# Rewriting the first attention of a two-layer network in fp32: narrow products, another split of the work over the engines

## What is computed

```python
xn = layernorm(x, axis=-1)                    # over the 512 columns
q  = xn.reshape(B, 8, 32, 512);  k = v = ctx.reshape(B, 8, 32, 512)
qk = einsum('bhdq,bhdl->bhql', q, k) / sqrt(32)
sm = softmax(qk, axis=-1)                     # over the 512 keys
x  = x + gamma * einsum('bhql,bhdl->bhdq', sm, v).reshape(B, 256, 512)
```

## Time and profile before

| | us |
|---|---|
| median of 3 runs | 2164.12 (2162.57 to 2165.21) |
| profiled execution | 2165.63 |
| its span | 2163.8 |
| first transposed score of tile 0, of tile 15 | 45.38, 489.10 |
| first product of the next stage | 527.39 |

### The profile page before, as it was taken

The page is one execution under the profiler, slowest core; times in us unless marked ns, Lnnn a source line. Parts: engine busy times, 40 slices in busy tenths (PEclk is TensorE's granted clock), DMA queues, the critical chain, the costliest instruction groups (busy, mean ns, idle before and its releaser), DMA issues. The chain is left out here.

```text
span 2163.8 us, 33174 instructions
## 1 busy us (share of the span) xinstructions
PE 1887.0 (87%) x10911; PEld 876.8 (41%) x11054; DVE 1692.2 (78%) x3042; ACT 1262.2 (58%) x2016; POOL 794.7 (37%) x681
## 2 busy tenths in 40 slices
PE   3998888896699999799398999999999997869998
PEld 0433333332244443354253444444444443324444
DVE  6799999998826637388688999999999994684443
ACT  2666666654534625144146999999999994521211
POOL 3112222212514515000202888888888883000000
PEclk9999999998899999899698999999999998889999
DMA  6754334402000000110001555555555656000000
GB/s 136 231 115 87 72 67 84 84 9 81 0 0 1 0 0 1 65 33 29 25 0 40 108 108 104 108 108 108 108 105 109 108 106 219 5 1 20 20 20 20
DMA packets 343369, 143.06 MB, mean 66 GB/s; under 512 B 307408, under 2 KB 315600, under 8 KB 342096
## 3 DMA queue, kind: packets, MB, share of 16 engines
q1 hardware_dynamic: 343248, 141.51, 29.5%
HBM read 70.15 MB, written 4.19 MB: 34 GB/s over the span
## 5 line engine op out<-in xcount | busy, mean ns | idle before, releaser
L1385 ACT ACTIVATE a_prob<-a_psS,a_bias,q_scale 128x1024 uint8<-128x1024 f32 x512 | 610.6, 1209 | 26.6 <-PE a_psS L1278 25.6
L1314 DVE TENSOR_REDUCE a_tops<-a_psM 128x1 f32<-128x512 f32 x1024 | 622.7, 681 | 2.0 <-PE a_psM L1268 0.4
L1364 POOL CAST a_wide<-a_pairs 128x2048 int16<-128x2048 uint8 x256 | 481.0, 1894 | 97.3 <-DMA a_pairs<-a_prob 84.8
L1268 PE MATMUL a_psM<-KT,QO 128*128 128x512 bf16 x968 | 353.5, 387 | 16.0 <-DVE a_tops L1314 10.3
L1278 PE MATMUL a_psS<-KT,QO 128*128 128x512 bf16 x967 | 292.9, 380 | 6.6 <-ACT a_prob L1385 3.6
L561 PE MATMUL psO<-prob,vs 128*128 128x512 f32 x512 | 267.2, 604 | 25.3 <-ACT prob L361 20.6
L1290 PEld LDWEIGHTS a_psO<-V,a_wide 128*128 128x128 f16 x4096 | 175.3, 96 | 144.3 <-DVE QO L1327 23.0
L361 ACT ACTIVATE prob<-psT 128x512 f32<-128x512 f32 x256 | 150.7, 595 | 127.1 <-PE psT L549 113.4
L675 POOL TENSOR_TENSOR g_sum<-g_sum 128x512 f32<-128x512 f32 x88 | 126.9, 1442 | 196.9 <-DVE g_sum L740 196.9
L1290 PE MATMUL a_psO<-V,a_wide 128*128 128x32 bf16 x4096 | 181.3, 177 | 20.3 <-DVE QO L1327 15.6
L849 PE MATMUL g_psY<-raw_dn,g_hT 128*128 128x512 f32 x352 | 162.2, 622 | 26.2 <-DVE raw_dn L700 15.8
(11 more groups left out here) (194 smaller groups left out, 2892.4 us busy)
## 6 DMA issues: line engine op xcount, KB each, us to landing
xs<-in_x SPq DMA_DIRECT2D x64, 256.0 KB, 4.7
cs<-in_ctx SPq DMA_DIRECT2D x64, 256.0 KB, 7.7
KT<-in_w SPq DMA_DIRECT2D x2, 4096.0 KB, 21.0
raw_gu<-in_gu SPq DMA_DIRECT2D x4, 1408.0 KB, 17.4
vs<-in_ctxT SPq DMA_DIRECT2D x64, 64.0 KB, 2.2
k_cT<-in_ctxT SPq DMA_DIRECT2D x16, 256.0 KB, 2.7
a_pairs<-a_prob SPq DMA_TRANSPOSE x256, 2.7
out<-x_sb SPq DMA_DIRECT2D x16, 256.0 KB, 2.0
```

Of the source, the lines that this page charges most:

```text
L1268: pe.matmul(psM[n % NM][:, :], QOf[:, i * P:(i + 1) * P], KTf[:, keys:keys + 512], start=True, stop=True).then_inc(shown, 1)
L1314: v.reduce_max(tops[i // JOIN % NB][:, i % JOIN, c:c + 1], psM[n % NM][:, :], AX.X).then_inc(topped, 1)
L1364: pool.tensor_copy(wide[i % NV][:, :, :, :].rearrange("p k c q -> p k (c q)"), both).then_inc(widened, 1)
L1385: act.activation(prob[i % NP][:, k * HK:(k + 1) * HK], psS[g % NS][:, :], ACT.Exp, scale=q_scale[:, i:i + 1], bias=bias[i // JOIN % NB][:, ...
```

## The change

The interface stays. In `mix_rows`:

- weigh now issues, for each quarter c of the keys, four fp32 products with a 32-column stationary operand (the head's values) into the four 32-partition pieces of one `psO`, and four with 32 columns of ones into `psE`: eight products per quarter, 32 a tile, where there were 16 with 128 columns. The pieces are ordered by quarter and then by head, and `prob` has eight slots.
- normalising moves to ACT (`Identity` with scale and bias, L441). ACT masks keys and queries directly (L434, L450), with no separate high copy; the subtraction for `ks` and `qs` is on POOL, head by head (L363, L372). The Newton step goes to POOL (L346 to L355).
- the maxima are split by one cast on DVE and three steps on POOL. One transpose turns all 48 columns; `less` (51 by 128 for each piece, with minus ones) picks and subtracts them in four 128-column products (L621) in place of one with 512 columns. `psS` has three buffers.
- collect runs once a tile, on 128 partitions, inside the following tile. Queries and keys are prepared two tiles ahead (three buffers), statistics three ahead. Unpacking is spread over the last two tiles. The loop is written out, and `vs` is loaded by one DMA a tile.

```diff
-    FIRST = 6
+    RING = 2 * HT
+    FIRST, LEAD = 3, 3
@@ gpsimd
+            def queries(j):
+                if j >= 3:
+                    pool.wait_ge(tscored, NU * (j - 2))
+                for h in range(HT):
+                    pool.wait_ge(q_cut, 2 * j + h // 2 + 1)
+                    pool.tensor_tensor(qs[j % 3][:, h, :], xs[j % 3][:, h, :], q_sub[:, h, :],
+                                       ALU.subtract).then_inc(q_ready, 1)
...
+            def steps(j):
+                if has(j - 2):
+                    finish(j - 2)
+                if has(j + 2):
+                    keys(j + 2)
+                if has(j + 3):
+                    roots(j + 3)
+                if has(j + 1):
+                    split(j + 1)
+                if has(j + 2):
+                    queries(j + 2)
@@ scalar
+            def steps(j):
+                for n in range(NU):
+                    if has(j):
+                        exp(j, n)
+                    if n in (0, 1) and has(j + 2):
+                        cut_keys(j + 2, n)
+                    if n == HT - 1 and has(j - 1):
+                        collect(j - 1)
+                    if n == 5 and has(j + 3):
+                        roots(j + 3)
+                    if 6 <= n < 6 + HT and has(j + 2):
+                        normalise(j + 2, n - 6)
+                    if n in (10, 11) and has(j + 2):
+                        cut_queries(j + 2, n - 10)
@@ vector
+            def steps(j):
+                if has(j + 3):
+                    statistics(j + 3)
+                if has(j + 1):
+                    maxima(j + 1)
+                if has(j - 1):
+                    invert(j - 1)
+                if has(j + 1):
+                    maxima_rows(j + 1)
+                if has(j - 2):
+                    after(j - 2)
+                if j == NT - 2:
+                    move(0)
+                    move(1)
+                    mask(0)
+                    mask(1)
...
@@ tensor
-                pe.matmul(psT[n % 2][:, :], neg1[:, :],
-                          mrow[b][:, h * LC:(h + 1) * LC, :].rearrange("p a b -> p (a b)"),
-                          start=False, stop=True).then_inc(tscored, 1)
+                for q in range(LC):
+                    mm = pe.matmul(out[:, q * P:(q + 1) * P], less[:, h * LC + q, :], mrow[j % 2][:, :],
+                                   start=False, stop=(q == LC - 1))
+                mm.then_inc(tscored, 1)
...
-                pe.matmul(psO[h % 2][:, :], vs[b][:, c, h, :], prob[:, n % 4, :],
-                          start=(c == 0), stop=(c == LC - 1)).then_inc(pv_done, 1)
+            def weigh(j, c):
+                if c == 0:
+                    pe.wait_ge(v_in_s[j % 2], 16 * (j // 2 + 1))
+                    if j:
+                        pe.wait_ge(o_read, 2 * j)
+                pe.wait_ge(exped, NU * j + HT * (c + 1))
+                for h in range(HT):
+                    pe.matmul(psO[h * D0:(h + 1) * D0, :], vs[j % 2][:, c, h * D0:(h + 1) * D0],
+                              prob[:, (c * HT + h) % RING, :], start=(c == 0), stop=(c == LC - 1))
+                for h in range(HT):
+                    pe.matmul(psE[h * D0:(h + 1) * D0, :], env["ones_f"][:, 0:D0],
+                              prob[:, (c * HT + h) % RING, :], start=(c == 0),
+                              stop=(c == LC - 1)).then_inc(pv_done, 1)
...
+            def steps(j):
+                for n in range(NU):
+                    if has(j):
+                        tscore(j, n)
+                    if has(j + 1) and FIRST <= n < FIRST + NU // 2:
+                        score(j + 1, 2 * (n - FIRST))
+                        score(j + 1, 2 * (n - FIRST) + 1)
+                    if has(j) and n > 1 and n % HT == 1:
+                        weigh(j, n // HT - 1)
+                if has(j + 1):
+                    turn_maxima(j + 1)
+                if has(j):
+                    weigh(j, LC - 1)
```

More of the change, by code:

```diff
@@ L241, in mix_rows @@
         rinv = sb("rinv", [P, DM], F32)
-        psS = [pb(f"psS{i}", [P, DM], F32) for i in range(2)]
+        psS = [pb(f"psS{i}", [P, DM], F32) for i in range(3)]
         psT = [pb(f"psT{i}", [P, DM], F32) for i in range(2)]
[L245 to L249, removed]
@@ L348, in _ @@
+            def steps(j):
[7 more added lines that the diff above has]
+                    split(j + 1)
+                if has(j + 2):
+                    queries(j + 2)
+            turns(steps)
+            finish(NT - 2)
+            finish(NT - 1)
         @block.scalar
@@ L468, in after @@
-            def after(j):
-                wait_before(v, added, j + 1, dve_passed)
-                v.bn_stats(env["stats"][:, j, :] if isinstance(j, int) else
-                           flat(env["stats"][:, :, :])[:, bass.ds(j * 6, 6)],
-                           flat(x_sb[:, :, :])[:, bass.ds(j * DM, DM)]).then_inc(after_s, 1)
-            def turn(j, b, first=False, more=True, done=True):
-                queries(j + 1, 1 - b)
-                for h in range(HT):
-                    maxima(j + 1, 2 * h, 2 * h + 2)
-                    if more:
-                        statistics(j + 2, b, h)
-                for h in range(HT):
-                    maxima(j + 1, 2 * (HT + h), 2 * (HT + h) + 2)
-                    if not first:
-                        invert(j - 1, 1 - b, h)
-                split_maxima(j + 1)
-                if more:
-                    variances(j + 2)
-                if done:
-                    after(j - 2)
-                maxima_rows(j + 1, 1 - b)
@@ L491, in _ @@
-            v.wait_ge(masks, 9)
-            for h in range(HT):
-                statistics(0, 0, h)
-            variances(0)
-            queries(0, 0)
-            maxima(0, 0, NU)
-            split_maxima(0)
-            maxima_rows(0, 0)
-            for h in range(HT):
-                statistics(1, 1, h)
-            variances(1)
-            turn(0, 0, first=True, done=False)
-            turn(1, 1, done=False)
-            in_pairs(v, turn, 2, NT - 2)
-            turn(NT - 2, 0, more=False)
@@ L517, in _ @@
                 v.tensor_scalar(env["w_gu"][:, g, :], env["raw_gu"][:, g, :].bitcast(F32), 2.0 ** 126, None,
                                 ALU.mult)
-            after(NT - 3)
-            for h in range(HT):
-                invert(NT - 1, 1, h)
+            def steps(j):
+                if has(j + 3):
+                    statistics(j + 3)
[12 more added lines that the diff above has]
+                    mask(1)
+                if j == NT - 1:
+                    move(2)
+                    move(3)
+                    scale(0)
+                    scale(1)
+                    mask(2)
+                    mask(3)
+                    scale(2)
+                    scale(3)
@@ L522, in _ @@
+            v.wait_ge(masks, 11)
+            turns(steps)
+            invert(NT - 1)
             after(NT - 2)
```

457 lines of the change are left out of this document (232 added, 225 removed).

## The result

| | before | after |
|---|---|---|
| median, us | 2164.43 (2162.57 to 2165.21) | 2105.66 (2104.2 to 2109.2) |
| profiled execution, and its span | 2165.63, 2163.8 | 2106.02, 2104.3 |
| first transposed score of tile 0, of tile 15 | 45.38, 489.10 | 44.03, 431.75 |
| from one tile's first transposed score to the next one's, mean of 15 | 29.58 | 25.85 |
| first product of the next stage | 527.39 | 466.76 |

The ratio is 0.9732, with a 95% interval of 0.9715 to 0.9749: faster by 58.8 us, where 100 had been forecast (2064). All of the gain lies in the rewritten stage: the next stage starts 60.6 us earlier, and what follows that point takes 1.1 us longer than before. A mean is that of all 15; a middle tile is one of the 13 between the first and the last of them.

A forecast was written before the change was run, and what follows sets the result against it. PE and DVE, both nearly full, were taken to wait for each other. Tiles going from 29.58 to 22.9 us gave -100 us, start +1, end -1.3, so 2165.6 became 2065, median 2064; range 2034 to 2176.

The forecast's parts named there:

- The lower end: Weighing: a group of eight 32-column fp32 products runs four abreast, twice, in 1.7 us; chance of four abreast 0.50.
- 3.4 us in strict order: Rival for weighing: products start strictly in order, 0.43 us each, a group 3.4; no gain on PE, 2165 us; chance 0.18.
- 6.9 one after another: Rival for weighing: 32-column products into one bank don't run abreast, a group takes 6.9 us; 2386 us; chance 0.12.
- the likeliest case: Four abreast in weighing: 22.9 us a tile, 2064 us, between 2040 and 2090; chance 0.50.
- part of the way: Rival: four abreast with a dearer start or slow POOL steps, 24.5 to 28 us a tile, 2090 to 2142; chance 0.14.
- the dearer start of a group: Weighing: one of two reasons given for 24.5 to 28 us a tile; the walk itself added 0.15 us for each group.
- slow small steps on POOL: POOL's ten new small steps near their upper bound, 1.30 us each instead of 0.25, making POOL 25 us a tile.
- the price of the subtraction: PE, subtracting maxima: four 128-column products take 0.26 us against 0.22, +0.8 us a tile, offset by -1.0 from fewer transposes.
- The clock: I add nothing: PE busy for about 80% of a tile; the granted clock was taken to stay at 1.00, adding no time.
- The stretch that it rested on: 1920 to 1940 us of the kernel before: PE busy 15.57 of 20 us, granted clock 1.00.
- The walk: One tile followed in order through PE's groups and ACT's exponentials, masks and normalising steps: 22.9 us a tile, mostly set by ACT.
- Start and end: First transposed score near 46.4 us, +1 us; last reciprocals 24.7 us into tile 15 instead of 26.0, -1.3 us.

The follow-up runs named there:

- run 3: The changed kernel with each group's eight products issued as values, ones, values, ones, head by head, instead of four and four: 2107.17 us in one run.
- run 1: The changed kernel with less and mrow filled up with zeros from 51 to 128 partitions: 2067.81 us, 0.9554 of before.
- run 8: The changed kernel with filled partitions, ACT's side work moved to where PE is busy, and the x_sb load cut into seven DMAs: 2045.36 us, 0.9445 of before.
- run 7: The kernel before with the narrow products alone; queries, Newton step and maxima stay on DVE: 2178.31 us, 1.006 of before.

## Why the prediction was right in sign and off in size

**Weighing.** The lower end was right: four abreast, twice. The group took 1.86 us and not 1.7, because 0.10 us is lost behind it, before the next full-width product starts: a turn like those of L621. Both other prices, 3.4 us in strict order and 6.9 one after another, fall with the 1.86 us; run 3 adds that later products pass earlier ones. The recorded sentence that all products of the kernel before use the whole width is not quite right, since its transposes L568 have 3 columns, but no two of them stand in different columns, so it changes nothing.

**The case.** 2105.66 us and 25.85 us a tile do not lie in the likeliest case (2040 to 2090, chance 0.50) but in "part of the way" (24.5 to 28 us a tile, 2090 to 2142, chance 0.14). Of that case's two reasons one, the dearer start of a group, gives 0.4 us a tile, and the other, slow small steps on POOL, did not happen. So the range held in good part by luck: what filled it, the turns of the subtraction and the clock, stands in none of the cases. (The three chances for faster, the same and slower add up to 1.01, a slip.)

**The step that failed** is the price of the subtraction: "four products of 128 columns with their own weights: 4 x 0.066 = 0.26 against 0.22, +0.8 us. Both together are nothing. What is left besides weighing is 11.2 us". The four products themselves take no more than one of 512 columns (they start 0.056 apart, and 0.22 go by in run 1), but the row used for them was of 128 partitions, and these have 51. From the transposed score to the end of the subtraction is 0.65 us a piece and not 0.44, 16 times a tile: 3.4 us, and with the groups PE needed 16 x 0.65 + 16 x 0.22 + 4 x 1.86 + 0.3 = 21.7 us and not 18.0. Run 1 takes that away and lands at 23.28 us a tile, where the forecast had 22.9, and at 2067.8, where it had 2064. But of the 3.4 us only about 1.0 lengthens a tile by itself; the rest falls into PE's waits for ACT.

**"The clock: I add nothing"** is the second step that failed, and by the tiles the dearer one: 0.92 instead of 1.00, 1.6 us a tile. It is right once either the turns or the waits are gone. The stretch that it rested on belongs to another stage with full-width products only; that it kept 1.00 with PE busy for 15.57 of 20 us said nothing about this one.

**The walk.** It had PE wait for ACT only ahead of the groups and at piece 13. The row at 151.12 shows 0.80 us of waiting for an exponential behind a key mask, already in piece 3 (counted from 0), ahead of the first group. The masks cost 1.14 (forecast 1.13), normalising 0.81 and not 0.684: the row used had one operand from memory, L441 has two. The Trainium skill, "ScalarE: Activation LUTs", "What ACT_TABLE_LOAD costs", puts such an operand at about 93 ns. The trace agrees: 684 against 589 ns, so 95, for one, and 597 ns with none (L458) against 811 with two, though L441 also reads from another memory.

**DVE, ACT and POOL.** DVE 17.1 us and ACT 16.8 in a tile (forecast 18.3 and 18.4); ACT's instructions overlap at their ends, which a sum of lengths doesn't show. POOL's small steps 0.20 to 0.23 us (forecast 0.25), so POOL is 13.2 us and waits for DVE. The reciprocals were not held up by POOL: 0.91 each, as 0.94 before. Maxima took 683 ns, against 668 before.

**Start and end.** DVE's timeline of the changed kernel, to be set beside the earlier trace rows:

```profile
30.23 2.47 DVE L499 BATCH_NORM_STATS2 stats<-xs 128x6 f32<-128x512 f32 x4 [6.94 <-DMA xs<-in_x]
...
33.04 9.62 DVE L513 TENSOR_REDUCE rmax<-psS 128x1 f32<-128x512 f32 x16
42.69 0.18 DVE L517 CAST rparts<-rmax 128x17 bf16<-128x17 f32 x1
44.14 0.22 DVE L524 COPY mrow<-psM 51x128 bf16<-51x128 bf16 x1 [1.26 <-PE psM L645]
...
451.36 3.15 DVE L550 TENSOR_SCALAR w_gu<-raw_gu 128x2816 f16<-128x2816 f32 x2
454.43 3.37 DVE L533 RECIPROCAL rinv<-e_sums 128x128 f32<-128x128 f32 x4
```

The fifth load landed as forecast. The first transposed score stands at 44.03, not 46.4, since the maxima took 9.62 and the splitting and turning 1.3. The last reciprocals start right behind the unpacking, 22.7 us into the last tile (431.75 to 454.43), forecast 24.7. Together start and end gave 4.6 us where the sum had 0.3.

The sum by measured terms: 15 x (25.85 - 29.58) = -56.0, start -1.35, end -3.3 (35.0 us from the last tile's start to the next stage instead of 38.3): -60.6, as the next stage's start says. Against the forecast, the tiles are 15 x (25.85 - 22.9) = 44 us too long; start and end give back 4.3 and what follows takes 1.1 more, which leaves 41. Of the 44, about 21 are the clock (1.6 x 13), 14 the turns (1.04 x 13), and the rest is the walk and the first and last tiles. Filling up the partitions (run 1) brings back both.

**What stays open:** why the clock falls in most tiles and not in the fourth, which has the same waits and turns; what moving the work off DVE is worth without the turns; and why the seventh tile of run 8 waits for its keys.

## What to carry to other kernels

A product's price depends on what stands next to it: in a chain of short products keep the number of partitions of the weights and their columns the same, if need be by filling with zeros, and read starts, not lengths, to see the turns. When a mend also changes the clock, compare tiles of the same clock before you give its gain to one cause. Two engines that are both nearly full should be relieved together: here the narrow products by themselves gained nothing and cost 0.6%. And when a stage has become a quarter shorter or a consumer has moved forward in it, look for transfers that the old order covered.

## What was not expected of the hardware

- 0.10 to 0.11 us for each change between 128-partition and 51-partition weights, and between full-width and 32-column products; none with 128 by 128 throughout.
- Four fp32 products of 32 columns by 512 run in 0.89 us, where one of 128 columns takes 0.86: nearly fourfold, whichever way values and ones are interleaved. By the starts in run 3 each 32-column piece of the array behaves as a queue of its own.
- About 2 us of useless products a tile made the kernel 8.8 us faster (clock 1.00 in place of 0.92).
- DVE's reciprocals (0.91 us), statistics (0.67) and maxima (0.68) ran beside POOL at the pace of the earlier trace rows; a step on 4 columns in SBUF waited for POOL's instruction to end, 2.78 us in run 7.
